# An attention kernel on one core: transposed probabilities multiplied into the values four pairs at a time, most of them kept in the score slots they came from

## The reference

```python
q = _split_heads(query_antecedent @ Wq, h) * d_head ** (-0.5)
k = _split_heads(memory_antecedent @ Wk, h)
v = _split_heads(memory_antecedent @ Wv, h)
logits = jnp.einsum('bhqd,bhkd->bhqk', q, k) + bias
weights = jax.nn.softmax(logits, axis=-1)
x = jnp.einsum('bhqk,bhkd->bhqd', weights, v)
```

## Time and profile before

| | |
|---|---|
| median of 3 runs | 1025.89 us (1025.48 to 1026.36) |
| span of the profiled execution | 1023.7 us, first to last instruction |
| TensorE busy | 984.9 us, 96% of the span |
| VectorE, ScalarE, GpSimd busy | 611.0, 490.6, 260.7 us |
| share of TensorE in the chain that ended last | 85% |

### The profile page before, as it was taken

One profiled execution on the slowest core, in us unless ns is written; L12 is line 12 of the kernel. 1 busy time (PEld: TensorE's weight loads), 2 busy tenths in 40 slices (PEclk: granted clock), 3 DMA queues, 4 the chain that ended last, 5 costly groups with the idle time before them and its releaser, 6 DMA issues.

```text
span 1023.7 us, 18213 instructions
## 1 busy us (share of the span) xinstructions
PE 984.9 (96%) x7322; PEld 808.5 (79%) x7330; DVE 611.0 (60%) x1183; ACT 490.6 (48%) x633; POOL 260.7 (25%) x254
## 2 busy tenths in 40 slices
PE   7999999999999999999999999977999999999996
PEld 5887777887777888777888777553589999999995
DVE  5616985465986376987363986588852112455552
ACT  3211886162786146687151588568721102355552
POOL 1201830001840000750000770488501101111100
PEclk9999999999999999999999999999999999999998
DMA  8192861522871613880521886400069959599930
GB/s 287 52 192 66 191 163 56 200 83 78 191 189 46 272 42 128 190 209 10 196 70 39 185 178 223 189 6 1 21 212 378 378 181 338 201 378 353 339 115 14
DMA packets 77596, 169.92 MB, mean 166 GB/s; under 512 B 6472, under 2 KB 17608, under 8 KB 72384
## 3 DMA queue, kind: packets, MB, share of 16 engines
q1 hardware_dynamic: 75392, 163.87, 52.4%
q0 software_dynamic: 2112, 4.80, 2.1%
HBM read 119.01 MB, written 16.10 MB: 132 GB/s over the span
## 4 chain that ended last, share of the span: by engine, by line
PE 85%; POOL 5%; DVE 3%; DMA 3%; issue 3%; ACT 1%; SPq 0%; POOLq 0%; DVEq 0%; ACTq 0%
PE psum L477 11%; PE psum L2274 9%; PE psum L457 7%; PE psum L492 7%; PE psum L2289 6%; PE psum L402 6%; PE psum L403 6%; PE psum L404 6%; PE psum L385 5%; PE psum L386 5%; PE psum L387 5%; DMA xg<-xm_rows,row_id 2%; PE psum L2306 2%; PE psum L2308 2%; PE psum L2307 2%
## 5 line engine op out<-in xcount | busy, mean ns | idle before, releaser
L917 POOL CAST stack<-kT 128x2048 fp32r<-128x2048 f32 x32 | 63.9, 2002 | 404.4 <-DVE keys_lo L611 392.9
L658 DVE CUSTOM_DVE_ANT_0 prob<-psum,biasmap,top 128x512 f32<-128x512 f32 x192 | 144.2, 751 | 21.2 <-PE psum L457 11.5
L826 ACT ACTIVATE prob<-prob,top 128x2048 f32<-128x2048 f32 x64 | 128.6, 2009 | 26.6 <-DVE top L658 26.3
L477 PE MATMUL psum<-ident,prob 128*128 128x128 f32 x1024 | 134.9, 275 | 1.2 <-issue 0.8
L2274 PE MATMUL psum<-xT,wring 128*128 128x128 f32 (+3 forms) x1024 | 134.0, 291 | 0.4 <-ACT xT L2628 0.4
L477 PEld LDWEIGHTS psum<-ident,prob 128*128 128x128 f32 x1024 | 116.2, 141 | 22.4 <-issue 7.7
L2274 PEld LDWEIGHTS psum<-xT,wring 128*128 128x128 f32 x1024 | 130.4, 191 | 1.8 <-ACT xT L2628 0.7
L788 ACT COPY kT<-psum 128x512 f32<-128x512 f32 x64 | 37.2, 586 | 191.5 <-PE psum L387 191.5
L834 ACT COPY probT<-psum 128x1024 f32<-128x1024 f32 x96 | 96.5, 1010 | 46.9 <-PE psum L492 45.2
L402 PE MATMUL psum<-wv_hi,ctx_part 128*128 128x512 f32 x256 | 100.0, 390 | 0.0
L403 PE MATMUL psum<-wv_lo,ctx_part 128*128 128x512 f32 x256 | 99.8, 390 | 0.0
(11 more groups left out here) (271 smaller groups left out, 1740.0 us busy)
## 6 DMA issues: line engine op xcount, KB each, us to landing
wring<-in_w SPq DMA_DIRECT2D x64, 1024.0 KB, 9.0
ctx_raw<-in_ctx_t SPq DMA_DIRECT2D x15, 1024.0 KB, 5.5
stack<-stack SPq DMA_DIRECT2D x32, 256.0 KB, 4.7
early_stack<-early_stack SPq DMA_DIRECT2D x28, 256.0 KB, 5.2
prob<-in_w_gate_t SPq DMA_DIRECT2D x1, 5632.0 KB, 17.2
stack<-key_stack SPq DMA_DIRECT2D x20, 256.0 KB, 4.2
query_stacks<-prob SPq DMA_DIRECT2D x16, 256.0 KB, 5.4
qstack<-query_stacks SPq DMA_DIRECT2D x16, 256.0 KB, 5.4
```

The costliest lines, as they stand in the source:

```text
L477: mm = pe.transpose(psum[:, w + i, j * P:(j + 1) * P], prob[:, prob_slot(n, j), kt * P:(kt + 1) * P], ident[:, :])
L658: dve.tensor_tensor_reduce(prob[:, slot, keys], psum[:, scores.of[n, j, c], :], biasmap[:, keys], 1.0, top[:, h, (c + 1) % 2:(c + 1) % 2 + ...
L826: act.activation(prob[:, slot, :], prob[:, slot, :], ACT.Exp, bias=top[:, h, 1:2], scale=-1.0, accum_out=top[:, h, 2:3]).then_inc(*raised. ...
```

## The change

Transposed pairs are no longer weighed one in each slot. In the slots four pairs are weighed together, in every fourth slot (slots 3 and 7 of a quad); in the tail two pairs are turned and then two weighed, by turns. To hold so many pairs, pairs 2, 3, 4 and 7 of a quad are moved into parts of the quad's own slots in `prob` whose keys have already been turned; pairs 0, 1, 5 and 6 go to the two places of `probT`. The moves of pairs 0 and 1 wait for pairs 5 and 6 of the quad before, those of 5 and 6 for pairs 0 and 1 of their own; the other four wait for no multiplication. The bias step that writes again into a quad's first or third slot waits for the multiplications that read there, and the load of the ternary weights into `prob` waits for a batch's last multiplication in place of its last transpose. At a batch's end the next key tile stands before the last two weighings.

```diff
+TOGETHER = 4
-        def steps_of_slot(n, i):
+        def step_of_slot(n, i):
             t = SLOTS_OF_QUAD * (n % DT - 1) + i - TURN_LATER
-            return (t if t >= 0 else None), (t - WEIGH_LATER if t >= WEIGH_LATER else None)
+            return t if t >= 0 else None
+        def weighed_behind(t):
+            if t not in TAIL:
+                return range(t - TOGETHER - 1, t - 1) if t % TOGETHER == 1 and t > TOGETHER else ()
+            return range(t - 3, t - 1) if t % 2 else ()
+        def turned_pair(n, p):
+            first = prob_slot(n, 0)
+            if p in (0, 1, 5, 6):
+                return probT[:, p % 5 if p < 6 else 1, :].rearrange("p (i j q) -> p i j q", i=2, j=QUAD)
+            if p == LAST:
+                return prob[:, first + QUAD - 1, HALF:].rearrange("p (i j q) -> p i j q", i=2, j=QUAD)
+            head, lo = first + (0 if p == 2 else 2), CHUNK if p == TOGETHER else 0
+            return prob[:, head:head + 2, lo:lo + CHUNK].rearrange("p i (j q) -> p i j q", j=QUAD)
+        def turned_place_free(n, p):
+            if p < 2:
+                return multiplied.at(n - 1, p + 5) if n else None
+            return multiplied.at(n, p - 5) if p in (5, 6) else None
...
-            def turn_and_weigh(b, turned_step, weighed_step):
-                if turned_step is not None:
-                    turn_pair(*pair_of_step(b, turned_step))
-                if weighed_step is not None:
-                    multiply_pair(*pair_of_step(b, weighed_step))
+            def turn_and_weigh(b, t):
+                turn_pair(*pair_of_step(b, t))
+                for weighed in weighed_behind(t):
+                    multiply_pair(*pair_of_step(b, weighed))
...
-                multiply_pair(*pair_of_step(b, STEPS - 2))
                 project_key_tile(b + 1, 0, 0)
+                multiply_pair(*pair_of_step(b, STEPS - 2))
                 multiply_pair(*pair_of_step(b, STEPS - 1))
...
                 elif g >= 2 and j == 0:
-                    dve.wait_ge(*turned.at(n - 2, 2 * c + 1))
+                    dve.wait_ge(*(turned.at(n - 2, 2 * c + 1) if c else multiplied.at(n - 2, PAIRS // 2 - 1)))
+                elif g >= 2 and (j, c) == (2, 0):
+                    dve.wait_ge(*multiplied.at(n - 2, LAST))
...
                 if tile == window.load_at:
-                    sp.wait_ge(*turned.at(DT * b - 1, LAST))
+                    sp.wait_ge(*multiplied.at(DT * b - 1, LAST))
```

More of the change, by code:

```diff
@@ L485, in multiply_pair @@
                     pe.wait_ge(*weighted.at(n - 1))
+                weights = turned_pair(n, p)
                 for kt in (2 * p, 2 * p + 1):
@@ L490, in multiply_pair @@
                         columns = slice((QUAD * g + j) * DH, (QUAD * g + j + 1) * DH)
-                        at = (kt % 2 * QUAD + j) * P
                         mm = pe.matmul(quad_out[j * DH:(j + 1) * DH, :], v[:, kt, columns],
-                                       probT[:, p % 2, at:at + P], start=(kt == 0), stop=(kt == KTILES - 1),
+                                       weights[:, kt % 2, j, :], start=(kt == 0), stop=(kt == KTILES - 1),
                                        tile_position=(0, j * DH))
@@ L559, in tensor_attention @@
                                 project_key_tile(b, CHUNKS - 1, which, (k,))
-                        if n > DT * b:
-                            turn_and_weigh(b, *steps_of_slot(n, i))
+                        step = step_of_slot(n, i)
+                        if step is not None:
+                            turn_and_weigh(b, step)
                         if n > DT * b and i == SUMS_AT:
@@ L567, in tensor_attention @@
                 for t in TAIL:
-                    turn_and_weigh(b, t, t - WEIGH_LATER)
+                    turn_and_weigh(b, t)
                     if t == STEPS - 3:
                         turn_sums(DT * (b + 1) - 1)
+                project_key_tile(b + 1, 0, 0)
                 multiply_pair(*pair_of_step(b, STEPS - 2))
-                project_key_tile(b + 1, 0, 0)
                 multiply_pair(*pair_of_step(b, STEPS - 1))
@@ L663, in move_pair @@
             def move_pair(n, p):
-                w = pair_bank(p)
-                before = pair_before(n, p, 2)
+                w, free = pair_bank(p), turned_place_free(n, p)
                 dve.wait_ge(*turned.at(n, p))
-                dve.wait_ge(*multiplied.at(*before))
-                dve.tensor_copy(probT[:, p % 2, :], psum[:, w:w + 2, :].rearrange("p a n -> p (a n)")).then_inc(
-                    *moved_v.made(n, p))
+                if free:
+                    dve.wait_ge(*free)
+                dve.tensor_copy(turned_pair(n, p), psum[:, w:w + 2, :].rearrange(
+                    "p i (j q) -> p i j q", j=QUAD)).then_inc(*moved_v.made(n, p))
             def spread_sums(n):
@@ L759, in vector_attention @@
                             add_bias(n, j, c)
-                        step = steps_of_slot(n, i)[0] if n > DT * b else None
+                        step = step_of_slot(n, i)
                         if step is not None and by_vector(*pair_of_step(b, step)):
@@ L829, in move_pair @@
             def move_pair(n, p):
-                w = pair_bank(p)
+                w, free = pair_bank(p), turned_place_free(n, p)
                 act.wait_ge(*turned.at(n, p))
[L832 to L835, removed]
+                if free:
+                    act.wait_ge(*free)
+                act.copy(turned_pair(n, p), psum[:, w:w + 2, :].rearrange(
+                    "p i (j q) -> p i j q", j=QUAD)).then_inc(*moved_a.made(n, p))
             for k in range(DT):
@@ L1312, in tensor_recurrence @@
             turn_tail(22)
+            turn_tail(23)
             multiply_tail(20)
-            turn_tail(23)
             multiply_tail(21)
             turn_tail(24)
+            turn_tail(25)
             multiply_tail(22)
-            turn_tail(25)
             multiply_tail(23)
             turn_tail(26)
+            turn_tail(27)
             multiply_tail(24)
-            turn_tail(27)
             multiply_tail(25)
@@ L1325, in tensor_recurrence @@
             add_attention_early(0)
+            turn_tail(29)
             multiply_tail(26)
-            turn_tail(29)
             multiply_tail(27)
@@ L1333, in tensor_recurrence @@
             add_attention_early(2)
+            turn_tail(31)
             multiply_tail(28)
-            turn_tail(31)
             multiply_tail(29)
```

2 lines of the change are left out of this document (removed).

## The result

The changed kernel takes **1031.19 us** (median of 8 runs, 1030.76 to 1036.34) against 1026.18 for the kernel before beside it (8 runs): a ratio of 1.005, 95% interval 1.0034 to 1.0065. It is slower by 5.0 us; forecast were 5.6. The profiled execution has a span of 1029.5 us, 5.8 above the 1023.7 of before.

What follows compares the result with a forecast made beforehand. TensorE was taken as the bound, VectorE only 1.51 us a quad behind. Slots losing 2.91 a batch, less tails gaining 1.55 (1.4 in the last), added 5.6 to 1025.9: 1031.5 us, range 1024 to 1037.

Steps and rivals of the forecast that it cites:

- Place and sign: Slots lose 2.91 us a batch up to the tail; tails gain 1.55, or 1.4 in the last batch.
- The block's chain: From slot 7's waited-for bias step to the next quad's first: 4.56 us, leaving VectorE idle 1.46; slot 3's chain 4.70.
- the bounds: Margins on the slots' sum: shorter first bias steps, a later matmul start, multiplications at 0.40 each; loss 2.0 to 3.4 a batch.
- A saved break: Each avoided switch between 128 x 128 and 128 x 32 tiles saves TensorE 0.31 us, 0.16 plus 0.15.
- Quad: Quads 2 and 3 take 17.92 us against 16.93, +0.99 each; quad 1 loses 0.93.
- head 0 with its move: VectorE's four bias steps and finish of head 0 plus one pair move: 3.10 + 1.13 = 4.23 us.
- Sum: Three batches lose 1.36 us each and the last 1.5, 5.6 in all, giving 1031.5 us.
- TensorE's busy share: In quads 2 and 3 TensorE is busy near 15 of about 17.9 us, its scores waiting for bias steps.
- The queue of DMA: Ternary weights issued some 4.5 us later, the largest landing 17.2 us after issue, about in time: costs nothing.
- TensorE stays the bound: Rival, chance 0.04: all 80 saved breaks count, 25 us less, 1001.
- VectorE without gaps: Rival, chance 0.08: VectorE bounds quads 2 and 3 at 15.42 us, 1004; decided when its stored work covers the block.
- More waits by ScalarE: Rival, chance 0.15: moves waiting within blocks delay exponentials, 0.4 us for each of 20 blocks, 8 more, 1039.

Runs made afterwards that it cites:

- Experiments 1: The changed kernel with its slots weighed one pair at a time again, tails still in twos: 1020.10 us against 1026.71 for the kernel before, ratio 0.9938.
- 2: The changed kernel with blocks of four in the slots, but tails, last batch and batch end ordered as before: 1038.58 us, ratio 1.011 to the kernel before.
- 3: The changed kernel with slots weighing blocks of two pairs in every second slot, tails as in the change: 1015.04 us, ratio 0.9888 to the kernel before.
- 7: The changed kernel with two score banks in place of three in batches 0 to 2: 1058.77 us, ratio 1.0309 to the kernel before.
- 9: The changed kernel, blocks of four, VectorE moving pair 5 in place of pairs 3 and 7: 1016.05 us against 1026.23 for the kernel before, ratio 0.9912.
- 10: The changed kernel, blocks of four, as with pair 5 alone but VectorE moving pair 7 instead: 1024.55 us, ratio 0.9986 to the kernel before.

## Why the prediction was right

- **Place and sign.** Slots lose, tails win, the slots by more. Experiments 1 and 2 show it part by part (-6.6 and +11.9 us). The forecast had 3 x 1.55 + 1.4 = 6.05 less for the tails and 4 x 2.91 = 11.6 more for the slots.
- **The block's chain** of 4.56 us measured 4.58 (141.86 to 146.44), with the pieces as forecast: 1.08 from bias step to transposes (0.81 + 0.27), 0.97, 1.88, 0.65. Slot 3's 4.70 measured 4.70. Four multiplications in one go ran at the pace forecast, and not at the 0.40 each that the bounds allowed for. That the length of the block against the stored work decides is shown from three sides: a shorter block (3), fewer banks (7), and a work that fills the wait at no cost (9 against 10).
- **A saved break:** 0.31 forecast, 0.29 measured by adding breaks, and 1.50 for five in the tail, 0.30 each. A tail's round took 2.90 for 2.89.
- **Quad:** 18.02 and 18.05 for 17.92, quad 1 +0.86 for +0.93. The term mis-sized is head 0 with its move: 4.23 forecast, 4.43 measured. I had taken 3.10 for every head from head 1; but the later bias steps of head 0 carry a third wait, and it takes 3.29 to its move (128.41 to 131.70), head 2 2.99 (137.54 to 140.53), so that its part is 4.32 for 4.43. The second error takes back half of the first.
- **Sum.** A batch takes 157.86 us for 156.36 before (99.18 to 572.77 and 99.59 to 568.66 for three): a loss of 1.51 for 1.36. The last one loses 1.91 for 1.5: its slots 3.12, and its tail gives 1.21 in place of 1.4 (637.57 to the recurrence's transposes at 664.07, against 630.34 to 658.05 before), as the wait for GpSimd ahead of the last multiplication grew from 0.24 to 0.54 (without it, the tail would have given 1.51). Against that, batch 0 begins 0.41 earlier, which is scatter (its first score starts at 98.8 to 99.95 in the 14 traces), and what follows the attention is 0.22 shorter, for which I have no cause. 3 x 1.51 + 1.91 - 0.41 - 0.22 = 5.8, the difference of the spans. So the closeness of 5.6 is in part luck: the batches lose 6.4, some 0.8 more than forecast, and 0.6 comes back from outside them.
- **TensorE's busy share** I put "near 15 of about 17.9"; the row says 16.52. The work is 15.07 as forecast, but half of the waiting (18.02 - 15.07 = 2.95, of which 1.50 shows) doesn't show as idle. A part lies within groups of two scores, which are drawn out from 0.71 to 1.10 (142.00); another behind single scores, whose rows last 0.48 to 0.51 where a score takes TensorE 0.27. A waiting engine can look busy in this view.
- **The queue of DMA.** Nothing, as forecast, though from a wrong pair of rows: the 5632 KB load is the gate's, of batch 2, and the sum at 198.64 reads batch 1's smaller ones. The gate's load, issued at 340.51, lands 16.0 us later, 1.1 ahead of the first sum over it, which begins right behind the value copy ahead of it (357.03, 357.64).

```profile
prob<-in_w_gate_t SPq DMA_DIRECT2D x1, 5632.0 KB, 16.0
```

```profile
357.03 0.69 DVE L636 COPY v<-psum 128x512 f32<-128x512 f32 x1 [2.03 <-PE psum L424]
357.64 3.07 DVE L726 TENSOR_REDUCE col<-prob 128x1 f32<-128x2816 f32 x1
```

- **Rivals.** TensorE stays the bound: no, it waits 28.5 us for bias steps. VectorE without gaps: no, 2.57 us of gaps a quad (1.50 + 1.07), and the experiments show the condition named for it, a shorter chain, to be the one that decides. More waits by ScalarE: it does wait longer for multiplications (3.1 us in quad 3, 2.2 before), but TensorE feels 4.5 us of it in the whole kernel.

What stays open: the 0.22 us behind the attention; a fourth bank; and whether the copies beside GpSimd's instructions are held by them, since no run took those away.

## What to carry to other kernels

Joining work of one kind saves what the change of kind costs, but a block interrupts the supply of the engine behind it. Before choosing the block's length, take its chain, from the step that frees a buffer to the first new result (4.56 us for four), less what the consumer does meanwhile (3.10, and in slot 3 the finish besides): that is the consumer's idle time for the block. All of a quad's idle times together must stay under the consumer's slack, here TensorE's 16.93 less VectorE's 15.42, or 1.51. Blocks of four leave 2.57, and lose; blocks of two leave 0.82, and win, although their chain of 3.70 too is longer than 3.10. Blocks of two gave up a third of the slots' saving and won 11.7 us; blocks of four lost 5. Where a long block must stay, put into it the work that the waiting engine has anyway: the same copy was free there, and cost 1.13 us a quad elsewhere.

## What the runs showed of the hardware

A change of tiles from 128 x 128 to 128 x 32 and back costs 0.29 to 0.31 us of TensorE, and a change from transposes to scores with the same tiles 0.01. A VectorE instruction that waits for a third semaphore, already reached, follows 0.1 us later (0.89 for 0.79; two such waits taken off shortened the quad by 0.18). A copy of VectorE's within SBUF that takes 0.23 alone lasts, beside an instruction of GpSimd's, until 0.07 to 0.09 behind that one's end, 1.90 us at most (62 copies in 14 traces).
